# Weight sums of the last down projection: accumulating DMAs from GpSimd's queue in place of VectorE, and two forms swapped

## Chip, cores and metric

The kernel runs on one core of one Trainium2 chip. The metric is the device time of one execution in microseconds, the median of the runs shown. All arithmetic is float32: a matmul operand is split into a rounded part ("hi", float32r) and the remainder ("lo", float32r), and every product is three matmuls (hi·hi, lo·hi, hi·lo).

## What is computed

```python
# x: (8, 128, 512), that is 1024 tokens of width 512
def _L0_cond_ref(...):                       # F = 1376, LoRA of rank 16 per batch entry
    gate = lora_add(einsum('bnh,fh->bnf', x, W_gate), x, A_gate, B_gate)
    up = lora_add(einsum('bnh,fh->bnf', x, W_up), x, A_up, B_up)
    return lora_add(einsum('bnf,hf->bnh', silu(gate) * up, W_down), act, A_down, B_down)
def _L0_ffn_ref(x, ln_w, gate_w, up_w, down_w):   # I = 1792
    nx = x * rsqrt(mean(x * x) + 1e-5) * ln_w
    g, u = nx @ gate_w.T, nx @ up_w.T
    return (silu(g) * u) @ down_w.T
x = x + _L0_ffn_ref(_L0_cond_ref(x, ...), ...)
```

Only the last line of `_L0_ffn_ref`, the product with `down_w`, is touched by the change.

## The kernel before

Channels stand on the 128 partitions and tokens along the free axis, in two halves of 512. Every large product is done by a Strassen-Winograd scheme: seven products of blocks in place of eight, for which sums of weight blocks and sums of activation blocks are made first. The program is one hand-written instruction stream for each engine, synchronised by semaphores, and each engine takes its stream strictly in the order written. In outline: gate and up of the first stage (groups `j` of 0 to 9), its down projection, the norm, gate and up of the second stage (groups `j` from `S1` on, in `group(j, ...)`), and last the down projection of the second stage.

The last down projection is a row of 49 *items* on TensorE, seven products of seven (`KF`) items; item `i` belongs to product `i // 7` and has `k = i % 7`. An item is six matmuls of 128x512: two output tiles by three passes. `DOWN` names each product's activation form, the number of its weight form, and its PSUM banks. Products 0, 5 and 6 use weight blocks as loaded (`vj_in`, tile `jraw`); products 1 to 4 (`nt1`, `nt2`, `22`, `t3`) use sums of blocks, of which there are four forms for each `k`, held in the tile `vs`.

How the forms of one `k` come to be: SP loads four blocks (512 KB) into `vraw`, a view of the tile `wdr` (`load_v`, L356). VectorE makes the four forms in place, four dependent additions of 128x256 (`sums_v`, L1012). ScalarE writes the rounded part of all four, 128x1024, to `vs` (`hi_v`, through the helper of L415), and VectorE the remainder (`lo_v`, through the helper of L889). There is one `vraw`, so the load of the next `k` waits for `lo_v` of the one before. This happens seven times, in the order `V_ORDER`. The first five of them lie in the groups of gate and up: `sums_v` in one group, `hi_v` on ScalarE at the same group's end, `lo_v` in the next group. The sixth ends among the first items, and the seventh (`k` = 6) is written out like this:

```python
                if i == 2 * KF - 1:
                    hi_v(KF - 1)        # ScalarE, behind its work for item 13
...
                elif i == 2 * KF - 1:
                    sums_v(KF - 1)      # VectorE, behind its work for item 13
                    lo_v(KF - 1)
```

TensorE waits for the `lo` of that `k` at the items of product 1 (`s_vlo`), so item 13 is the first to use the seventh set. Behind `hi_v(KF - 1)` stand on ScalarE `copy_q1()` and the rounded operand of item 14 (`hi_down(14)`); behind `lo_v(KF - 1)` stand on VectorE the sum (`down_sum("nt2", 0)`, L1035) that `hi_down(14)` reads, and the remainder `lo_down(14)`. Item 14 waits for both. `load_v(KF - 1)` stands on SP behind `lo_v` of the sixth set; `copy_u2()` puts two PSUM banks into `wdr` much later.

GpSimd makes a mask and a few zeros in the first part of the program and has nothing after that.

Of the kernel before, what the change touches and what calls it, by code (L numbers as in the profile page):

```python
# [16 lines left out]
P = 128  # L17
# [6 lines left out]
S1, S2 = G1 - 2, G2 - 2  # L24
# [7 lines left out]
KF = FF // 2  # L32
# [6 lines left out]
V_ORDER = (4, 5, 0, 1, 2, 3, 6)  # L39
# [2 lines left out]
RING_F = (X11, XT1, XT2, X21, X22, XT3, XT4)  # L42


def build(nc, xT_in, idx_in, wsh_in, w0_in, wgu_in, wd_in, vs_in, vj_in, agu_in, bgu_in, ad_in, bd_in, lnw_in, out):
    f32, f32r, i32 = mybir.dt.float32, mybir.dt.float32r, mybir.dt.int32
    ALU, ACT = mybir.AluOpType, mybir.ActivationFunctionType
    ds = bass.ds
    ctx = ExitStack()
    with ctx:  # L50
# [3 lines left out]
        def sem(name):  # L54
            return ctx.enter_context(nc.semaphore(name))
# [78 lines left out]
        DA_BANK, DB_BANK, DG_BANK = [bank[3], bank[7]], [bank[0], bank[2]], [bank[5], bank[1]]  # L134
# [25 lines left out]
        vraw = wdr[:, :, :].rearrange("p a n -> p (a n)").rearrange("p (c m) -> p c m", m=256)  # L160
# [9 lines left out]
        def act_at(f, t):  # L170
            return act[:, f, t * CH:(t + 1) * CH]
# [5 lines left out]
        def slot_f(u, part):  # L177
            s = u % 14
            return xs[:, RING_F[s // 2], part, s % 2, :]

        DOWN = (("11", None, 0, DA_BANK), ("nt1", 3, None, DG_BANK), ("nt2", 1, None, DB_BANK), ("22", 2, None, DG_BANK),
                ("t3", 0, None, DB_BANK), ("21", None, 1, DA_BANK), ("t4", None, 2, DB_BANK))

        def down_op(i):
            name, k = DOWN[i // KF][0], i % KF
            return act_at(k + KF if name in ("21", "22") else k, 0 if name in ("11", "t3", "21") else 1)

        def down_w(i, part):
            form, j = DOWN[i // KF][1:3]
            return vs[:, i % KF, form, part, :] if j is None else ws[:, j % 2, i % KF, part, :]  # L190
# [11 lines left out]
        def w_of(g):  # L202
            return g + 2
# [57 lines left out]
        s_var, s_rs, s_nw, s_nx = sem("var_done"), sem("rsqrt_done"), sem("refine_steps"), sem("nx_done")  # L261
        s_ug, s_uu, s_us, s_um = sem("unit_gate"), sem("unit_up"), sem("unit_silu"), sem("unit_act")
        s_z, s_pre, s_res = sem("last_product"), sem("residual_with_copy"), sem("residual_added")
        s_v_ld, s_vsum, s_vhi, s_vlo = sem("v_loaded"), sem("v_sums"), sem("v_hi"), sem("v_lo")
        s_j_ld, s_jhi, s_jlo = sem("j_loaded"), sem("j_hi"), sem("j_lo")
        s_dsum, s_dca, s_dcm, s_dcu = sem("down_sums"), sem("down_q1_copied"), sem("down_g_copied"), sem("down_u2_copied")

# [126 lines left out]
        def _(pool):  # L394
# [14 lines left out]
            pool.wait_ge(s_stklo, 8)  # L409
            nc.gpsimd.memset(ad[:, :, :, RANK:2 * RANK], 0.0).then_inc(s_ad_pad, 1)  # L410

        @block.scalar
        def _(a):
            def copy(out_ap, in_ap, scale=1.0):
                return nc.scalar.activation(out_ap, in_ap, ACT.Copy, scale=scale)  # L415
# [135 lines left out]
                copy(wdc[:, n, 0, :], wdr[:, n % 2, :]).then_inc(s_wdhi, 1)  # L551

            def hi_v(k):
                a.wait_ge(s_vsum, 4 * k + 4)
                copy(vs[:, V_ORDER[k], :, 0, :], vraw).then_inc(s_vhi, 1)

            def hi_j(n):
# [31 lines left out]
            def hi_down(i):  # L589
                name, k = DOWN[i // KF][0], i % KF  # L590
                if name in ("11", "22", "21"):
                    a.wait_ge({"11": s_c11[1], "22": s_c22f, "21": s_c21[1]}[name], S1 // 2 + k + 1)
                else:
                    a.wait_ge(s_dsum, ("nt1", "nt2", "t3", "t4").index(name) * KF + k + 1)
                if i >= 14:
                    a.wait_ge(s_use, 11 + i - 13)
                elif i % 2 == 0:
                    a.wait_ge((s_q1, s_g, s_p6, s_q2, s_p3, s_p7, s_p4)[i // 2], S2)
                copy(slot_f(i, 0), down_op(i)).then_inc(s_ahi, 1)
# [267 lines left out]
            for i in range(2, 7 * KF):  # L867
                p = i // KF
# [18 lines left out]
        def _(v):  # L887
            def sub(out_ap, raw, part):
                return nc.vector.tensor_tensor(out_ap, raw, v32(part), ALU.subtract)  # L889
# [83 lines left out]
            def stack_lo(c, t):  # L973
                v.wait_ge(s_stkhi, 4 * c + 2 * t + 2)
                part = (slice(2 * t, 2 * t + 2), slice(0, CHUNK[c]))
                sub(stk[c % 2][32:64, part[0], part[1]], raw[c % 2][0:32, part[0], part[1]],
                    stk[c % 2][0:32, part[0], part[1]]).then_inc(s_stklo, 1)
# [26 lines left out]
                v.wait_ge(s_wdhi, n + 1)  # L1004
                sub(wdc[:, n, 1, :], wdr[:, n % 2, :], wdc[:, n, 0, :]).then_inc(s_wdlo, 1)

            def sums_v(k):
                v.wait_ge(s_v_ld, 16 * (k + 1))
                for q, (to, more) in enumerate(((3, 0), (0, 1), (1, 3), (2, 1))):
                    if q >= 1:  # L1010
                        v.wait_ge(s_vsum, 4 * k + q)
                    nc.vector.tensor_tensor(vraw[:, to, :], vraw[:, to, :], vraw[:, more, :], ALU.add).then_inc(s_vsum, 1)  # L1012

            def lo_v(k):
                v.wait_ge(s_vhi, k + 1)
                v.wait_ge(s_vsum, 4 * k + 4)
                part = vs[:, V_ORDER[k]]
                sub(part[:, :, 1, :], vraw, part[:, :, 0, :]).then_inc(s_vlo, 1)

# [28 lines left out]
            def lo_down(i):  # L1048
                name, k = DOWN[i // KF][0], i % KF
                v.wait_ge(s_ahi, 22 + i + 1)  # L1050
                if name in ("nt1", "nt2", "t3", "t4"):
                    v.wait_ge(s_dsum, ("nt1", "nt2", "t3", "t4").index(name) * KF + k + 1)
                sub(slot_f(i, 1), down_op(i), slot_f(i, 0)).then_inc(s_alo, 1)
# [131 lines left out]
            def group(j, first, last):  # L1185
                if j > first:
                    if j not in (1, S1 + 2, S1 + 3):
                        c22_sum(j - 1)
                    if 1 <= j < 7:
                        stack_lo((j - 1) // 2 + 2, (j - 1) % 2)  # L1190
                    if j % 2 == 0:
                        c22_act(j - 1)
                if w_next(j) < last:
                    sums(w_of(w_next(j)))
                if j > S1 + 2 and j % 2 == 0:
                    lo_v((j - S1) // 2 - 2)
                elif j > S1 + 2:
                    sums_v((j - S1) // 2 - 1)
                if j > first and j % 2 == 0:
                    c21(j - 1)  # L1200
                if w_next(j) < last:
                    lo_a(w_of(w_next(j)))
                    if j == 0:
                        x_sum(0, 3)
                    elif j == S1 + 2:
                        c12(j)
                        c22_sum(j)
                    lo_b(w_of(w_next(j)))
                if j == 0:
                    c22_sum(0)  # L1210
                    lo_t(0, 3)
                if j >= S1 and j % 2 == 0:
                    down_sum("nt1", (j - S1) // 2 - 1)
                if j == S2 - 1:
                    lo_down(0)
                    lo_down(1)
                    lo_j(0)
                    lo_j(1)
                if j == S1 - 1:
                    lo_wd(0)  # L1220
                    lo_ac(0)
                if j % 2 == 1 and j != S1 + 3:
                    c11(j)
                if j != S1 + 2:
                    c12(j)
# [91 lines left out]
            for i in range(2, 7 * KF):  # L1317
                p, k = i // KF, i % KF
                if i % KF == 0 and p == 4:
                    for h in range(4):  # L1320
                        with_copy(h, *((s_dcu, du2, ALU.add) if h < 2 else (s_dcm, dm5, ALU.subtract)))
                elif i % KF == 0 and p == 5:
                    for h in range(2):
                        residual(h, 3, DG_BANK, ALU.add, False)
                elif i % KF == 0 and p == 6:
                    for h in range(2, 4):
                        residual(h, 4, DB_BANK, ALU.subtract, False)
                if p in (2, 4, 6) and k == 0:
                    down_sum(("nt2", "t3", "t4")[p // 2 - 1], 0)
                if p in J_AT:  # L1330
                    lo_j(KF * J_AT.index(p) + k)
                if p in (2, 4, 6) and k + 1 < KF:
                    down_sum(("nt2", "t3", "t4")[p // 2 - 1], k + 1)
                lo_down(i)
                if i == 3:
                    c22_act(S2 - 1)
                elif i == 4:
                    c21(S2 - 1)
                elif i == 5:
                    lo_v(KF - 2)  # L1340
                elif i == KF - 1:
                    down_sum("nt1", KF - 1)
                elif i == 2 * KF - 1:
                    sums_v(KF - 1)
                    lo_v(KF - 1)
            for h in range(2):
                residual(h, 5, DA_BANK, ALU.add, True)
# [9 lines left out]
        def _(pe):  # L1357
# [343 lines left out]
            def down_item(i, tiles=range(2)):  # L1701
                p, k = i // KF, i % KF
                for h in tiles:
                    for s, r in PASSES:
                        ins = mm(DOWN[p][3][h][:, :], down_w(i, s)[:, h * P:(h + 1) * P], slot_f(i, r),  # L1705
                                 start=(p < 2 and k == 0 and s == 0 and r == 0),
# [108 lines left out]
```

## Time and profile before

| | us |
|---|---|
| Median of 3 runs | 396.95 (396.59 to 397.47) |
| Span of the profiled execution | 395.5 |
| Runs' median less that span | 1.45 |
| TensorE busy | 391.8 |
| VectorE busy | 314.8 |
| ScalarE busy | 240.8 |
| GpSimd busy | 10.6 |

The profile is of one execution; its own time is known as its span, from the first instruction to the last, and the median of the runs stands 1.45 us above it. Sums below are made on the span and carried over to the median. Matmuls are pipelined and their ends are modelled, so that busy 99% of the span means that the profile shows no gap between matmuls, not that the array is at its peak.

### The profile page before, as it was taken

The numbers are of one execution on the slowest core, as the hardware profiler recorded it, in microseconds if no ns is written. First come the engines' busy times: TensorE is split into PE (matmuls) and PEld (weight loads), VectorE is DVE, ScalarE is ACT, GpSimd is POOL, SyncE is SP. The second block draws the span as 40 slices with busy tenths as digits, with TensorE's granted clock in tenths as the row PEclk, the third lists the DMA queues.
The fourth block names the chain that finished last, engine by engine and source line by source line (L and its number), as shares of the span: only waits on it lengthen the run. The fifth ranks groups of instructions, "written<-read, shape, count | busy, mean of one in ns | idle before, by whom it ended". The sixth has DMA issues, their size and how long they took to land.

```text
span 395.5 us, 5733 instructions
## 1 busy us (share of the span) xinstructions
PE 391.8 (99%) x1984; PEld 327.3 (83%) x1984; DVE 314.8 (80%) x476; ACT 240.8 (61%) x386; POOL 10.6 (3%) x13
## 2 busy tenths in 40 slices
PE   9999999999999999999999999999999999999997
PEld 5899888888888888888888888888888888888885
DVE  4899979586835869578699787878787869899994
ACT  5969786857574469815745656464646494484740
POOL 6300000000000000000000000000000000000000
PEclk9999999999999999999999999999999999999999
DMA  7640243311111551000400021313130316105112
GB/s 271 182 133 0 83 133 98 110 53 55 53 55 54 164 154 57 2 0 0 159 2 1 12 97 55 106 53 108 60 119 37 89 57 199 55 1 201 54 53 108
DMA packets 14942, 32.42 MB, mean 82 GB/s; under 512 B 2370, under 2 KB 4930, under 8 KB 14914
## 3 DMA queue, kind: packets, MB, share of 16 engines
q1 hardware_dynamic: 13792, 30.22, 23.7%
q10 hardware_dynamic: 1122, 1.84, 1.3%
q8 instruction: 16, 0.26, 0.3%
q14 instruction: 12, 0.10, 0.1%
HBM read 29.95 MB, written 2.10 MB: 81 GB/s over the span
## 4 chain that ended last, share of the span: by engine, by line
PE 99%; DVE 0%; issue 0%; DVEq 0%
PE bank L1365 53%; PE bank L1705 17%; PE bank L1593 14%; PE bank L1511 3%; PE bank L1557 3%; PE bank L1546 3%; PE bank L1375 3%; PE bank L1615 1%; PE bank L1607 1%; PE bank L1505 1%; PE bank L1714 0%; PE bank L1622 0%; DVE act L1354 0%; DVEq L1352 0%
## 5 line engine op out<-in xcount | busy, mean ns | idle before, releaser
L1365 PE MATMUL bank<-xs,ws 128*128 128x512 f32 x840 | 195.0, 390 | 0.0
L1365 PEld LDWEIGHTS bank<-xs,ws 128*128 128x128 f32 x840 | 156.6, 188 | 31.9
L415 ACT ACTIVATE xs<-act 128x512 fp32r<-128x512 f32 x71 | 42.8, 623 | 21.1 <-DVE act L1045 7.6
L1593 PE MATMUL bank<-xs,wdc 128*128 128x512 f32 x240 | 55.7, 390 | 0.0
L1593 PEld LDWEIGHTS bank<-xs,wdc 128*128 128x128 f32 x240 | 44.8, 188 | 9.5 <-issue 0.2
L889 DVE TENSOR_TENSOR xs<-act,xs 128x512 fp32r<-128x512 f32 x71 | 47.5, 685 | 2.7 <-ACT xs L415 2.1
L889 DVE TENSOR_TENSOR ws<-wraw,ws 128x256 fp32r<-128x256 f32 (+2 forms) x45 | 30.0, 668 | 13.0 <-ACT ws L415 12.8
L415 ACT ACTIVATE bank<-bank 128x512 f32<-128x512 f32 x30 | 17.3, 580 | 34.5 <-PE bank L1365 33.7
L415 ACT ACTIVATE mu<-bank 128x512 f32<-128x512 f32 x44 | 26.1, 596 | 20.1 <-PE bank L1365 13.6
L1705 PE MATMUL bank<-xs,vs 128*128 128x512 f32 x168 | 38.2, 389 | 0.0
L1705 PEld LDWEIGHTS bank<-xs,vs 128*128 128x128 f32 x168 | 31.5, 188 | 6.5
L889 DVE TENSOR_TENSOR ws<-wsum,ws 128x1024 fp32r<-128x1024 f32 x20 | 24.5, 1225 | 12.0 <-ACT ws L415 12.0
L415 ACT ACTIVATE ws<-wraw 128x256 fp32r<-128x256 f32 (+2 forms) x44 | 26.8, 614 | 7.8 <-PE bank L1365 3.3
L1705 PE MATMUL bank<-xs,ws 128*128 128x512 f32 x120 | 27.7, 389 | 0.0
L1705 PEld LDWEIGHTS bank<-xs,ws 128*128 128x128 f32 x120 | 22.5, 188 | 4.7
L415 ACT ACTIVATE stack<-bgu_raw 32x1024 fp32r<-32x1024 f32 (+1 forms) x20 | 22.7, 1137 | 0.3
L415 ACT ACTIVATE ws<-wsum 128x1024 fp32r<-128x1024 f32 x20 | 21.1, 1055 | 2.3 <-DVE wsum L903 2.3
L487 ACT ACTIVATE act<-bank 128x512 f32<-128x512 f32 (+1 forms) x28 | 16.3, 596 | 9.3 <-PE bank L1375 6.8
L1365 PE MATMUL bank<-xs,wx 128*128 128x512 f32 x84 | 19.7, 389 | 0.0
L1365 PEld LDWEIGHTS bank<-xs,wx 128*128 128x128 f32 x84 | 15.8, 188 | 3.3
L889 DVE TENSOR_TENSOR wdc<-wdr,wdc 128x512 fp32r<-128x512 f32 x10 | 6.9, 687 | 11.4 <-ACT wdc L415 11.4
L889 DVE TENSOR_TENSOR stack<-bgu_raw,stack 32x1024 fp32r<-32x1024 f32 (+1 forms) x10 | 13.2, 1322 | 2.9 <-ACT stack L415 2.7
(133 smaller groups left out, 439.5 us busy)
## 6 DMA issues: line engine op xcount, KB each, us to landing
wraw<-wgu_in SPq DMA_DIRECT2D x22, 512.0 KB, 3.3
wdr<-vs_in SPq DMA_DIRECT2D x7, 512.0 KB, 3.6
wraw<-vj_in SPq DMA_DIRECT2D x3, 896.0 KB, 4.7
wdr<-wd_in SPq DMA_DIRECT2D x10, 256.0 KB, 2.7
xa<-xT_in SPq DMA_DIRECT2D x4, 256.0 KB, 4.1
xa<-xT_in ACTq DMA_DIRECT2D x2, 512.0 KB, 4.7
bgu_raw<-bgu_in SPq DMA_DIRECT2D x32, 32.0 KB, 1.9
xres<-xT_in SPq DMA_DIRECT2D x4, 256.0 KB, 3.5
```

The costliest lines, as they stand in the source:

```text
L415: return nc.scalar.activation(out_ap, in_ap, ACT.Copy, scale=scale)
L487: return nc.scalar.activation(out_ap, in_ap, ACT.Silu, scale=scale)
L889: return nc.vector.tensor_tensor(out_ap, raw, v32(part), ALU.subtract)
L1365: ins = mm(z[:, :], w_slot(j)[:, w, s, k * P:(k + 1) * P], xs[:, c, r, k, :], start=(start and k == 0 and s == 0 and r == 0), stop=(k == 1 ...
L1375: ins = mm(z[0:m, half], stk[c % 2][:, 2 * t + q, cols], t_op[:, half], start=(alone and q == 0), stop=(q == 1), skip_group_check=True)
L1505: mm(B_BANK[i % 2][:, :].rearrange("p (k n) -> p k n", k=KT), one, one.unsqueeze(1).to_broadcast([P, KT, P]), start=True, stop=True)
L1511: mm(UNIT_BANK[i][g][:, cols], w0_tile(s, k, g, i), x_op(k, 0, r)[:, cols], start=(k == 0 and s == 0 and r == 0 and cols.start == 0), stop ...
L1546: mm(UNIT_BANK[n][g][:, :], w0_tile(s, k, g, UNITS[n][0]), x_op(k, 1, r), start=(k == 0 and s == 0 and r == 0), stop=(k == KT - 1 and s == ...
L1557: ins = mm(SHORT_BANK[t][g][:, half], wsh[s][:, k, g, q, :], x_op(k, t, r)[:, half], start=(k == 0 and s == 0 and r == 0 and q == 0), stop ...
L1593: ins = mm(z[:, :], wd[:, s, h * P:(h + 1) * P], x[r], start=(start and s == 0 and r == 0), stop=False, skip_group_check=True)
L1607: ins = mm(T_BANK[t][32 * b:32 * b + 32, tokens], ad[:, 2 * t + b // 2, n, col:col + 2 * RANK], act_at(ORDER_C[n], t)[:, tokens], start=(n ...
L1705: ins = mm(DOWN[p][3][h][:, :], down_w(i, s)[:, h * P:(h + 1) * P], slot_f(i, r), start=(p < 2 and k == 0 and s == 0 and r == 0), stop=(s ...
```

## The change

GpSimd takes over the weight sums. The host feeds a second array, `vmore_in`, three blocks (384 KB) for each `k`. After `load_v` has landed, GpSimd issues a DMA that adds these three blocks onto the first three of `vraw`, waits for it, and issues a second DMA that adds `vraw`'s second block, read twice, onto its third and fourth (256 KB written). The second DMA's semaphore is what `hi_v` and `lo_v` now wait for. `sums_v` and its three calls are gone from VectorE. The four forms stand in another order in `vraw`, so `nt1` uses form 1 and `nt2` form 3.

```diff
-        DOWN = (("11", None, 0, DA_BANK), ("nt1", 3, None, DG_BANK), ("nt2", 1, None, DB_BANK), ("22", 2, None, DG_BANK),
+        DOWN = (("11", None, 0, DA_BANK), ("nt1", 1, None, DG_BANK), ("nt2", 3, None, DB_BANK), ("22", 2, None, DG_BANK),
...
+            for k in range(KF):
+                pool.wait_ge(s_v_ld, 16 * (k + 1))
+                nc.gpsimd.dma_start(vraw[:, 0:3, :], vmore_in[V_ORDER[k]].rearrange("p (a m) -> p a m", a=3), accum_op=ALU.add
+                                    ).then_inc(s_vsum[0], 16)
+                pool.wait_ge(s_vsum[0], 16 * (k + 1))
+                nc.gpsimd.dma_start(vraw[:, 2:4, :], vraw[:, 1:2, :].to_broadcast([P, 2, 256]), accum_op=ALU.add
+                                    ).then_inc(s_vsum[1], 16)
...
             def hi_v(k):
-                a.wait_ge(s_vsum, 4 * k + 4)
+                a.wait_ge(s_vsum[1], 16 * (k + 1))
...
-            def sums_v(k):
-                v.wait_ge(s_v_ld, 16 * (k + 1))
-                for q, (to, more) in enumerate(((3, 0), (0, 1), (1, 3), (2, 1))):
-                    if q >= 1:
-                        v.wait_ge(s_vsum, 4 * k + q)
-                    nc.vector.tensor_tensor(vraw[:, to, :], vraw[:, to, :], vraw[:, more, :], ALU.add).then_inc(s_vsum, 1)
...
                 elif i == 2 * KF - 1:
-                    sums_v(KF - 1)
                     lo_v(KF - 1)
...
-        "vs_in": np.stack([blocks[b] for b in ((1, 0), (0, 0), (0, 1), (1, 1))], 2).reshape(KF, P, 4 * 256),
+        "vs_in": np.stack([blocks[b] for b in ((1, 0), (1, 1), (0, 1), (0, 0))], 2).reshape(KF, P, 4 * 256),
+        "vmore_in": np.stack([blocks[b] for b in ((0, 0), (1, 0), (0, 0))], 2).reshape(KF, P, 3 * 256),
```

VectorE's stream where the seventh set is made, before. The first row is the sum for item 13, the seven rows behind it are the remainders of items 7 to 13, and the rows of L1035 and what follows are sum and remainder for items 14 and on.

```order
L1030 TENSOR_TENSOR act<-act 128x512 [waits c12_act,c11_act]
L889 TENSOR_TENSOR xs<-act,xs 128x512 [waits down_sums,act_hi] x7
L1012 TENSOR_TENSOR wdr<-wdr 128x256 [waits v_loaded]
L1012 TENSOR_TENSOR wdr<-wdr 128x256 [waits v_sums] x3
L889 TENSOR_TENSOR vs<-wdr,vs 128x4x256 [waits v_sums,v_hi]
L1035 SCALAR_TENSOR_TENSOR act<-act 128x512 [waits c22_act,act_lo,act_hi] x2
L889 TENSOR_TENSOR xs<-act,xs 128x512 [waits down_sums,act_hi]
```

The same place of VectorE's stream in the changed kernel.

```order
L897 TENSOR_TENSOR xs<-act,xs 128x512 [waits act_hi]
L1031 TENSOR_TENSOR act<-act 128x512 [waits c12_act,c11_act]
L897 TENSOR_TENSOR xs<-act,xs 128x512 [waits down_sums,act_hi] x7
L897 TENSOR_TENSOR vs<-wdr,vs 128x4x256 [waits v_sums,v_hi]
L1036 SCALAR_TENSOR_TENSOR act<-act 128x512 [waits c22_act,act_lo,act_hi] x2
L897 TENSOR_TENSOR xs<-act,xs 128x512 [waits down_sums,act_hi]
```

The four additions are gone; nothing else on VectorE has changed its place. The remainder of the seventh set still stands ahead of everything for item 14, and its wait is now for a DMA.

GpSimd's stream in the changed kernel, from its last zeros on; before, it ended with the row of L410.

```order
L410 MEMSET ad 128x44x16 [waits stack_lo]
L414 DMA wdr<-vmore_in 128x768 [waits v_loaded]
L417 DMA wdr<-wdr 128x2x256 [waits v_sums_of_two]
L414 DMA wdr<-vmore_in 128x768 [waits v_loaded]
L417 DMA wdr<-wdr 128x2x256 [waits v_sums_of_two]
```

The pair of DMAs stands there seven times, and each DMA waits for the one before it to land.

## Rows read from the trace of the kernel before

**Rows 1.** The page: span, and busy time of each engine with its count of instructions.

```profile
span 395.5 us, 5733 instructions
PE 391.8 (99%) x1984; PEld 327.3 (83%) x1984; DVE 314.8 (80%) x476; ACT 240.8 (61%) x386; POOL 10.6 (3%) x13
```

**Rows 2.** Waits of TensorE, all of them: us in total, times, longest us.

```profile
PE bank L1505 <- PEq L1808: 0.8, 1, 0.8
```

**Rows 3.** The chain that ended last, in order of time: start us, us, what.

```profile
0.85 3.57 PE bank L1505 x8
...
194.71 129.95 PE bank L1365 x573
324.65 2.72 PE bank L1705 x12
...
328.73 62.56 PE bank L1705 x276
391.29 1.44 PE bank L1714 x12
```

**Rows 4.** Instructions on tile `wdr`: duration min/median/max ns, first and last start.

```profile
L1012 DVE TENSOR_TENSOR wdr<-wdr x28: 417/424/427, 226.4 to 338.7; 128x256 f32<-128x256 f32 x28
```

**Rows 5.** Timeline from 233 us, one of the first sets: start, us, what, [idle before].

```profile
233.66 0.33 SPq L356 DMA_DIRECT2D wdr<-vs_in  x1
...
241.14 1.79 DVE L1012 TENSOR_TENSOR wdr<-wdr 128x256 f32<-128x256 f32 x4
...
245.89 1.05 ACT L415 ACTIVATE vs<-wdr 128x1024 fp32r<-128x1024 f32 x1
...
249.89 0.58 ACT L415 ACTIVATE bank<-bank 128x512 f32<-128x512 f32 x1 [2.95 <-PE bank L1365]
```

**Rows 6.** SP's queue from 185 us: start, us, what.

```profile
237.81 9.85 SPq L282 DMA_DIRECT2D wraw<-wgu_in  x2
```

**Rows 7.** Timeline from 331 us, the seventh set: start, us, what, [idle before].

```profile
331.56 0.33 SPq L356 DMA_DIRECT2D wdr<-vs_in  x1
...
331.93 25.49 SPq L370 DMA_DIRECT2D wraw<-vj_in  x2
...
337.29 1.81 DVE L1012 TENSOR_TENSOR wdr<-wdr 128x256 f32<-128x256 f32 x4
339.13 1.06 ACT L415 ACTIVATE vs<-wdr 128x1024 fp32r<-128x1024 f32 x1 [5.39 <-DVE wdr L1012]
...
340.22 1.23 DVE L889 TENSOR_TENSOR vs<-wdr,vs 128x1024 fp32r<-128x1024 f32 x1 [1.13 <-ACT vs L415]
...
342.08 1.24 ACT L415 ACTIVATE xs<-act 128x512 fp32r<-128x512 f32 x2 [0.93 <-DVE act L1035]
342.75 0.69 DVE L889 TENSOR_TENSOR xs<-act,xs 128x512 fp32r<-128x512 f32 x1
```

**Rows 8.** DMAs issued, whole span: KB each, median us from issue to landing.

```profile
wdr<-vs_in SPq DMA_DIRECT2D x7, 512.0 KB, 3.6
wraw<-vj_in SPq DMA_DIRECT2D x3, 896.0 KB, 4.7
wdr<-wd_in SPq DMA_DIRECT2D x10, 256.0 KB, 2.7
...
act<-xT_in SPq DMA_DIRECT2D x4, 256.0 KB, 6.2
out<-xres SPq DMA_DIRECT2D x4, 256.0 KB, 2.0
```

**Rows 9.** DMAs issued from 325 to 345 us, same columns.

```profile
wraw<-vj_in SPq DMA_DIRECT2D x1, 896.0 KB, 8.9
wdr<-vs_in SPq DMA_DIRECT2D x1, 512.0 KB, 5.7
```

**Rows 10.** Stretches of the span: busy by engine (PE, PEld, DVE, ACT, POOL), PEclk, DMA share, GB/s.

```profile
337.29:339.10 1.81, 1.81 (x10) 1.50 (x9) 1.70 (x4) 0.00 (x0) 0.00 (x0) 1.00 0.28 112
...
395.00:395.50 0.50, 0.00 (x0) 0.00 (x0) 0.00 (x0) 0.00 (x0) 0.00 (x0) 0.50 0.00 0
```

More of the change, by code:

```diff
@@ L42, with build @@
 RING_F = (X11, XT1, XT2, X21, X22, XT3, XT4)
-def build(nc, xT_in, idx_in, wsh_in, w0_in, wgu_in, wd_in, vs_in, vj_in, agu_in, bgu_in, ad_in, bd_in, lnw_in, out):
+def build(nc, xT_in, idx_in, wsh_in, w0_in, wgu_in, wd_in, vs_in, vmore_in, vj_in, agu_in, bgu_in, ad_in, bd_in, lnw_in, out):
     f32, f32r, i32 = mybir.dt.float32, mybir.dt.float32r, mybir.dt.int32
@@ L263, in build @@
         s_z, s_pre, s_res = sem("last_product"), sem("residual_with_copy"), sem("residual_added")
-        s_v_ld, s_vsum, s_vhi, s_vlo = sem("v_loaded"), sem("v_sums"), sem("v_hi"), sem("v_lo")
+        s_v_ld, s_vsum, s_vhi, s_vlo = sem("v_loaded"), [sem("v_sums_of_two"), sem("v_sums")], sem("v_hi"), sem("v_lo")
         s_j_ld, s_jhi, s_jlo = sem("j_loaded"), sem("j_hi"), sem("j_lo")
@@ L1005, in lo_wd @@
                 sub(wdc[:, n, 1, :], wdr[:, n % 2, :], wdc[:, n, 0, :]).then_inc(s_wdlo, 1)
-            def sums_v(k):
-                v.wait_ge(s_v_ld, 16 * (k + 1))
-                for q, (to, more) in enumerate(((3, 0), (0, 1), (1, 3), (2, 1))):
-                    if q >= 1:
-                        v.wait_ge(s_vsum, 4 * k + q)
-                    nc.vector.tensor_tensor(vraw[:, to, :], vraw[:, to, :], vraw[:, more, :], ALU.add).then_inc(s_vsum, 1)
             def lo_v(k):
                 v.wait_ge(s_vhi, k + 1)
-                v.wait_ge(s_vsum, 4 * k + 4)
+                v.wait_ge(s_vsum[1], 16 * (k + 1))
                 part = vs[:, V_ORDER[k]]
@@ L1196, in group @@
                     lo_v((j - S1) // 2 - 2)
-                elif j > S1 + 2:
-                    sums_v((j - S1) // 2 - 1)
                 if j > first and j % 2 == 0:
```

## The prediction

> **What bounds the kernel.** I read the page first. TensorE is busy 391.8 of 395.5 us, VectorE 314.8, ScalarE 240.8, GpSimd 10.6 [rows 1]. The list of TensorE's waits has one entry, 0.8 us at the very start [rows 2]. The chain that ended last is TensorE's own stream: 573 matmuls in 129.95 us and 276 in 62.56 us, 0.2267 us each in both [rows 3]. So TensorE is never starved, and VectorE's load is not what the end waits for. Work taken off VectorE is worth nothing as long as that is so, and whatever makes TensorE wait is added whole, because no idle time behind it can absorb it.
>
> That turns the question into one of spare time: by when must each set of weight sums be there, and how much later does it come from two DMAs than from VectorE?
>
> **What is removed.** 28 additions of 0.424 us [rows 4], 11.9 us of VectorE in seven portions of 1.8 us. By the paragraph above this gives 0.0 on TensorE. The swap of forms 1 and 3 reads another slice of the same tile and costs nothing; all four forms of a `k` come from one ScalarE copy and one VectorE subtraction, before and after.
>
> **What is added, the first six sets.** Call C the time from the landing of `vs_in` to the landing of the second accumulating DMA. For the second set the load is issued at 233.66 and lands 3.6 later at its median [rows 5, 8], at about 237.3. ScalarE's copy of the sums starts at 245.89 [rows 5]. So C up to 8.6 us changes nothing at all. Behind the copy ScalarE has 2.95 us in which it waits for TensorE before its next copy, the one at 249.89 [rows 5], so C up to 11.6 is absorbed there. That next copy is awaited by TensorE only after two more products of six matmuls (2.72 us less the copy's 0.58, about 2.1), so TensorE itself first waits at C of some 13.7. The sets 3 to 5 repeat this pattern, the first is loaded during the norm, long before its sums at 226.4 [rows 4], and the sixth ends among items whose operands are made ahead. One thing works against it here: SP issues another weight load at 237.81 [rows 6], 512 KB, which runs on beside the first accumulating DMA. A load of that size takes 3.6 alone [rows 8], so sharing costs at most about that: with C of 8.6 it would be 12.2, still under 13.7. I cost these six at nothing; the cover is ScalarE's wait for TensorE.
>
> **What is added, the seventh set.** Here the cover is thin. An item is 6 x 0.2267 = 1.36 us. Item 2 begins at 328.73 [rows 3], so item 13 begins at 328.73 + 11 x 1.36 = 343.69 and item 14 at 345.05. Now [rows 7]: the load goes out at 331.56, VectorE's sums start at 337.29 when it has landed (5.7 us later [rows 9]), and end at 339.10; ScalarE copies at 339.13; VectorE's remainder runs 340.22 to 341.45, and item 13 may start, 2.24 us early. But item 14's operand is queued behind on both engines: its sum, ScalarE's copy at 342.08, VectorE's remainder at 342.75 to 343.44. That is 1.61 us ahead of item 14. From there on the chain makes an operand in 1.2 us, faster than TensorE's 1.36, so item 14 is the tightest place.
>
> The load's landing does not move: it is issued when the sixth set's remainder is done, and that stands behind work that waits for TensorE. So with C = 1.81 now, TensorE's stall is S = C - 1.81 - 1.61 = C - 3.42, of which C - 4.05 falls ahead of item 13 and up to 0.63 ahead of item 14.
>
> **How long is C?** No DMA of GpSimd's queue and no accumulating one is in this trace, so I bound it. *Below:* as if both were plain loads of SP. 256 KB take 2.7, 512 KB 3.6 [rows 8], 384 KB between them 3.15; together 5.85, S = 2.4. *Above:* 256 KB took 6.2 in a crowded moment, and 512 KB 5.7 [rows 8, 9]; one of each gives 11.9, S = 8.5. *Between:* an accumulating DMA also reads its destination. If that costs like twice the bytes, 384 KB become 768, between 512 at 3.6 and 896 at 4.7, so 4.3; 256 become 512, 3.6; with SP's issue time of 0.33 [rows 7] once for each, C = 8.6 and S = 5.2. I take this. The other end's cause is partly present: the 896 KB load issued at 331.93 lands only after 8.9 us, at 340.8 [rows 7, 9], and the DMA engines are still 28% busy from 337.29 to 339.10 [rows 10].
>
> The Trainium skill (DMA: Bandwidth & Descriptors, Anatomy of one DMA) fits a DMA from GpSimd as 2.0 us plus its bytes at 436 GB/s. By it the two would take 2.9 and 2.6, an estimate of C = 5.5 and S = 2.1; its figure for 256 KB agrees with the trace's 2.7, and it says nothing of accumulation.
>
> **The clock.** In the last half microsecond of the span the granted clock is 0.50, the level of 1.2 GHz [rows 10]; the last matmul ended at 391.29 + 1.44 = 392.73 [rows 3], so the clock fell within 2.3 us of idleness there. With C = 8.6 the idle time ahead of item 13 is 4.55 us, longer than that. The nearest price for coming back is the program's start, where 8 matmuls took 3.57 us, 0.446 each [rows 3], in place of 1.81 at 0.2267: 1.76 lost. Of that the 0.63 us which TensorE would wait ahead of item 14 anyway is absorbed, leaving 1.1. I add it. The Trainium skill (TensorE: Matmul & The Clock Gate, Why this matters for your kernels) has the rule that idle gaps between bursts of matmuls put the clock back to its lower level; the fall at the end of this span agrees.
>
> **Sum.** 0.0 for VectorE, 0.0 for six sets, 5.2 for the seventh, 1.1 for the clock: +6.3 us. On the profiled span 395.5 gives 401.8; on the median, 1.45 higher, 396.95 gives 403.3.
>
> **Rivals.**
>
> *The chain is longer than every cover* (10%). If an accumulating DMA of these sizes takes 7 us or more, C passes 13.7 in the groups too, where the load at 237.81 adds to it. At C = 15 in the groups each of the five sets 2 to 6 costs 1.3, together 6.5; the seventh costs 15 - 3.42 + 1.1 = 12.7; that gives 416. For it: nothing in the trace prices accumulation. Against: no load in [rows 8] has a median above 6.2.
>
> *No slower* (8%). The turning point is C = 3.4, or 4.2 if 0.2% (0.8 us, about what a measurement of this kernel can tell from no change) is allowed. The shortest landing for 256 KB is 2.0, a store [rows 8]; two DMAs at that speed make C = 4.0, a stall of 0.6 and 397.5. Against it: loads of the same size take 2.7, and there are two in a row here. A gain proper would need TensorE to have waited for VectorE, which its list of waits excludes [rows 2]; I leave 2% of the 8 for it, at 396.
>
> *Same chain, clock stays up* (within the forecast's 82%). If the gap ends before the clock falls, the sum is 5.2 and the time 402.2. If the DMAs are as quick as plain loads, the idle time ahead of item 13 is 1.8, shorter than the 2.3 at the span's end, and the time is 396.95 + 2.4 = 399.4.
>
> **Numbers.** Forecast 82% (the seventh set alone stalls, C from 5.85 to 12 or so), its own range 399.4 to 406.6 (8.5 + 1.1 above). The long chain has 10%; to leave out no more than two in ten I carry the upper end a little into the space between the two, to 409.5, and the lower end to 399.2. Slower 92%, within 0.2% 6%, faster 2%.
>
> **What would show it.** VectorE's rows of L1012 gone, its busy time down by about 12 us. Two GpSimd DMAs seven times, some 4 to 5 us from issue to landing each. ScalarE's copies to `vs` in the groups later by under 3 us, with no new wait on TensorE before 343 us. The seventh copy near 346, waiting for a DMA; TensorE's first wait inside the program at item 13, 4 to 5 us long, a shorter one at item 14; a granted clock below 1.00 behind it. I am wrong if TensorE waits in the groups (C above 13.7), if C is under 4.2, or if the load's landing at 337.29 moves.

## The result

The changed kernel takes 403.61 us (402.48 to 405.64, 5 runs) where the one before took 396.95: 1.0168 times as long, 95% interval 1.0142 to 1.0195. The forecast was 403.3. The profiled execution was the longest of the five, 405.64 with a span of 403.9; the other spans are 400.8 to 401.9. In the experiments two single executions far above all others of their kernel are left out as slow ones (1422.6 us in run 3, and 661.93 us in run 4, at a mean granted clock of 0.559).

The page of the changed kernel: span, busy time, two rows of the 40 slices, GpSimd's DMA queue, and the two new DMAs with KB each and median us to landing.

```profile
span 403.9 us, 5719 instructions
...
PE 393.7 (97%) x1984; PEld 328.6 (81%) x1984; DVE 303.6 (75%) x448; ACT 241.0 (60%) x386; POOL 25.7 (6%) x27
...
PE   9999999999999999999999999999999999399997
...
PEclk9999999999999999999999999999999999699999
...
q0 software_dynamic: 2912, 4.59, 6.9%
...
wdr<-vmore_in POOLq DMA_DIRECT2D x7, 384.0 KB, 5.8
...
wdr<-wdr POOLq DMA_DIRECT2D x7, 256.0 KB, 3.6
```

VectorE lost the 28 additions and 11.2 us [rows 1, 4], while GpSimd gained 15.1 us to issue the DMAs (10.6 before). TensorE has one slice in 40 (10.1 us each) in which it is busy for about a third, and in the same slice PEclk falls. The waits of TensorE, all of them (us in total, times, longest us), answer to [rows 2]:

```profile
PE bank L1703 <- DVE vs L897: 6.5, 1, 6.5
PE bank L1503 <- PEq L1807: 0.9, 1, 0.9
```

One new wait, for VectorE's remainder of the seventh set, at item 13. The timeline there, answering to [rows 7] (start, us, what, idle before; L423 and L897 are the helpers that were L415 and L889):

```profile
331.65 0.33 SPq L356 DMA_DIRECT2D wdr<-vs_in  x1
...
337.82 0.92 POOL L414 DMA_DIRECT2D wdr<-vmore_in  x1 [15.17 <-DMA wdr<-vs_in]
343.92 1.22 POOL L417 DMA_DIRECT2D wdr<-wdr  x1 [5.18 <-DMA wdr<-vmore_in]
347.59 1.06 ACT L423 ACTIVATE vs<-wdr 128x1024 fp32r<-128x1024 f32 x1 [13.76 <-DMA wdr<-wdr]
...
348.68 1.23 DVE L897 TENSOR_TENSOR vs<-wdr,vs 128x1024 fp32r<-128x1024 f32 x1 [11.30 <-ACT vs L423]
...
350.05 25.17 PE L1703 MATMUL bank<-xs,vs 128*128 128x512 f32 x102 [6.52 <-DVE vs L897]
```

C is read off here: the load has landed when GpSimd starts at 337.82, the second DMA has landed when ScalarE starts at 347.59, so C = 9.8 us. Item 12 ended at 343.53, item 13 begins at 350.05. In stretches of 1 us (busy of PE, PEld, DVE, ACT, POOL, then PEclk, DMA share, GB/s):

```profile
346.00:347.00 1.00, 0.00 (x0) 0.00 (x0) 0.00 (x0) 0.00 (x0) 0.00 (x0) 0.99 1.24 199
347.00:348.00 1.00, 0.00 (x0) 0.00 (x0) 0.00 (x0) 0.41 (x1) 0.00 (x0) 0.50 0.09 11
...
352.00:353.00 1.00, 1.00 (x4) 0.81 (x3) 1.00 (x2) 0.47 (x1) 0.00 (x0) 0.50 0.00 0
353.00:354.00 1.00, 1.00 (x4) 0.77 (x4) 1.00 (x3) 0.43 (x2) 0.00 (x0) 0.59 0.00 0
354.00:355.00 1.00, 1.00 (x6) 0.83 (x5) 1.00 (x3) 0.43 (x2) 0.00 (x0) 1.00 0.00 0
```

The granted clock is at 0.50, the 1.2 GHz level, from 347.0 to 353.8, and from 350.05 on matmuls run at it: 4 in a microsecond, not 6. The groups show the other half of the story, a chain with cover. The second set, answering to [rows 5]:

```profile
237.24 0.94 POOL L414 DMA_DIRECT2D wdr<-vmore_in  x1 [35.23 <-DMA wdr<-vs_in]
...
243.88 1.21 POOL L417 DMA_DIRECT2D wdr<-wdr  x1 [5.70 <-DMA wdr<-vmore_in]
...
247.66 1.06 ACT L423 ACTIVATE vs<-wdr 128x1024 fp32r<-128x1024 f32 x1 [1.82 <-DMA wdr<-wdr]
249.73 0.58 ACT L423 ACTIVATE bank<-bank 128x512 f32<-128x512 f32 x1 [1.01 <-PE bank L1363]
```

C is 10.4 here. ScalarE's copy comes 1.8 us late, its next wait for TensorE is 1.01 in place of 2.95, and TensorE notices nothing. The sixth set has a longer chain:

```profile
314.01 0.93 POOL L414 DMA_DIRECT2D wdr<-vmore_in  x1 [10.70 <-DMA wdr<-vs_in]
...
321.45 1.21 POOL L417 DMA_DIRECT2D wdr<-wdr  x1 [6.51 <-DMA wdr<-vmore_in]
...
325.11 1.06 ACT L423 ACTIVATE vs<-wdr 128x1024 fp32r<-128x1024 f32 x1 [2.31 <-DMA wdr<-wdr]
```

C is 11.1 there, and 9.7 to 11.4 over sets 2 to 6: the first DMA takes 6.1 to 7.4 us in these places and the second 3.6 to 4.4.

### The profile page after: what moved, and what is told of

It is laid out like the page before. It is cut to its first block, busy times and chain, and to the rows that moved or that the text cites. A ratio compares the mean times of both kernels' runs of the same rounds, so it can differ in the third digit from the quotient of the medians.

```text
span 403.9 us, 5719 instructions
## 1 busy us (share of the span) xinstructions
PE 393.7 (97%) x1984; PEld 328.6 (81%) x1984; DVE 303.6 (75%) x448; ACT 241.0 (60%) x386; POOL 25.7 (6%) x27
## 4 chain that ended last, share of the span: by engine, by line
PE 87%; DMA 6%; issue 3%; DVE 2%; ACT 1%; POOL 0%; DVEq 0%; ACTq 0%; POOLq 0%
PE bank L1363 46%; PE bank L1591 14%; PE bank L1703 12%; PE bank L1509 3%; PE bank L1555 3%; PE bank L1544 3%; PE bank L1373 3%; DMA wdr<-vs_in 2%; DMA wdr<-wdr 2%; DMA wdr<-vmore_in 2%; PE bank L1613 1%; PE bank L1605 1%; DVE vs L897 1%; PE bank L1503 1%; PE bank L1712 0%
## 5 line engine op out<-in xcount | busy, mean ns | idle before, releaser
L423 ACT ACTIVATE xs<-act 128x512 fp32r<-128x512 f32 x71 | 42.8, 623 | 19.0 <-DVE act L1046 7.6
L897 DVE TENSOR_TENSOR xs<-act,xs 128x512 fp32r<-128x512 f32 x71 | 47.6, 687 | 4.6 <-ACT xs L423 4.0
L1703 PE MATMUL bank<-xs,vs 128*128 128x512 f32 x168 | 40.3, 402 | 6.5 <-DVE vs L897 6.5
L897 DVE TENSOR_TENSOR ws<-wraw,ws 128x256 fp32r<-128x256 f32 (+2 forms) x45 | 30.0, 669 | 19.8 <-ACT ws L423 19.7
L1703 PEld LDWEIGHTS bank<-xs,vs 128*128 128x128 f32 x168 | 32.8, 196 | 13.9 <-issue 6.9
L423 ACT ACTIVATE mu<-bank 128x512 f32<-128x512 f32 x44 | 26.1, 596 | 19.5 <-PE bank L1363 13.0
L897 DVE TENSOR_TENSOR ws<-wsum,ws 128x1024 fp32r<-128x1024 f32 x20 | 24.5, 1225 | 12.0 <-ACT ws L423 12.0
L423 ACT ACTIVATE bank<-bank 128x512 f32<-128x512 f32 x30 | 17.3, 580 | 26.8 <-PE bank L1363 25.9
L423 ACT ACTIVATE ws<-wraw 128x256 fp32r<-128x256 f32 (+2 forms) x44 | 26.8, 614 | 7.8 <-PE bank L1363 3.3
L423 ACT ACTIVATE stack<-bgu_raw 32x1024 fp32r<-32x1024 f32 (+1 forms) x20 | 22.7, 1137 | 0.3
L423 ACT ACTIVATE ws<-wsum 128x1024 fp32r<-128x1024 f32 x20 | 21.1, 1054 | 2.5 <-DVE wsum L911 2.5
L423 ACT ACTIVATE vs<-wdr 128x1024 fp32r<-128x1024 f32 x7 | 7.4, 1062 | 25.0 <-DMA wdr<-wdr 25.0
L414 POOL DMA_DIRECT2D wdr<-vmore_in x7 | 6.6, 942 | 206.1 <-DMA wdr<-vs_in 206.1
```

What stands on the lines that cost most here:

```text
L414: nc.gpsimd.dma_start(vraw[:, 0:3, :], vmore_in[V_ORDER[k]].rearrange("p (a m) -> p a m", a=3), accum_op=ALU.add).then_inc(s_vsum[0], 16)
```

## The experiments

All were timed against the kernel before on the chip they ran on; ratios are to that, with 95% intervals. Times are medians. The recorded ratios agree with means over the executions other than the profiled one, so they can differ by some 0.2% from the ratio of two medians.

**1. The seventh set back on VectorE.** GpSimd keeps the first six.

```diff
-            for k in range(KF):
+            for done, k in enumerate(k for k in range(KF) if k not in ON_DVE):    # ON_DVE = (6,)
...
+                elif j > S1 + 2:
+                    sums_v((j - S1) // 2 - 1)          # does nothing unless k is in ON_DVE
...
                 elif i == 2 * KF - 1:
+                    sums_v(KF - 1)
                     lo_v(KF - 1)
```

> GpSimd's DMAs make the first six sets of weight sums, VectorE's four additions the seventh, in the block order of before. Theory (only the seventh set is exposed): the whole loss is gone, 396.9 us within 0.8 of before, no wait on TensorE inside the program. Rival (the first six sets, their DMA traffic or ScalarE's later copies cost too): 398 us or more, with a wait or longer matmul spacing between 226 and 343 us.

396.80 against 397.22, ratio 0.9993 (0.9984 to 1.0002). TensorE's only wait is the 0.9 us at the start. The whole loss is in the seventh set, and the six others cost nothing that shows.

**2. Only the seventh set on GpSimd.** The same kernel with `ON_DVE = (0, 1, 2, 3, 4, 5)`.

> VectorE makes the first six sets, GpSimd's DMAs only the seventh. Theory: the loss of the whole change, 402.5 to 404.5 us, one wait of about 5 to 6.5 us on TensorE at item 13. Rival (several sets share the loss): clearly less, 400 us or under.

405.02, ratio 1.0197 (1.0182 to 1.0212), a little above the range that I gave; its interval overlaps that of the changed kernel on another chip (run 9, 1.0155 to 1.0202). One wait on TensorE, 4.8 us; the clock is low behind it for longer than in the changed kernel, to 354.7.

```profile
342.50 1.20 POOL L423 DMA_DIRECT2D wdr<-wdr  x1 [4.24 <-DMA wdr<-vmore_in]
346.16 1.06 ACT L429 ACTIVATE vs<-wdr 128x1024 fp32r<-128x1024 f32 x1 [12.27 <-DMA wdr<-wdr]
...
348.62 3.75 PE L1721 MATMUL bank<-xs,vs 128*128 128x512 f32 x8 [4.78 <-DVE vs L903]
```

**3. The gap filled with matmuls.** Into bank 4, which no one uses between the gate and up products and the last items.

```diff
                 pe.wait_ge(s_alo, 22 + i + 1)
+                if i == 2 * KF - 1:
+                    pe.wait_ge(s_c21[0], S2 // 2)
+                    pe.wait_ge(s_c21[1], S2 // 2)
+                    for n in range(20):
+                        mm(bank[4][:, :].rearrange("p (k n) -> p k n", k=KT), one,
+                           one.unsqueeze(1).to_broadcast([P, KT, P]), start=True, stop=True)
```

> The changed kernel with 20 extra bf16 matmuls of 512 columns (4.3 us at full clock) that TensorE issues into an unused bank ahead of its wait for the seventh set; nothing else is different. Theory (the gap also costs a fall of the clock): granted clock 1.00 behind the gap, time down by 1.1 to 1.9 us against the changed kernel, so 401.7 to 402.5. Rival (the clock's fall costs nothing measurable, the wait is all): 403.6 as the changed kernel.

403.85, ratio 1.0158 (1.0137 to 1.0179): not faster than the changed kernel's 403.61, which had run on another chip. The mean granted clock was 1.00, so the fall was prevented and yet the time hardly moved. So I ran it again later, beside the changed kernel (9 and 10).

**4. The seventh set loaded early.** Into `wsum`, free once the last gate and up weights are made, instead of `wdr`.

```diff
+        vraws = [vraw] * (KF - 1) + [wsum[:, :, :]]
...
                 if j == 0:
+                    load_v(KF - 1)      # waits for the load before to land, not for lo_v
                     sp.wait_ge(s_c22f, S2 // 2)
...
-                    load_v(KF - 1)
```

> All seven sets by GpSimd's DMAs, but the seventh is loaded into the tile that held the gate and up sums (free from about 314 us on), some 17 us earlier, so that its chain of DMAs is over long before item 13. Theory (the DMAs cost only what their chain is late): 396.9 us within 0.8 of before, no wait on TensorE. Rival (the DMAs themselves slow something, or the seventh chain delays the sixth): 398 or more.

397.41 against 397.22, ratio 1.0005 (0.9996 to 1.0014), no wait on TensorE in the program. All fourteen DMAs are there and cost nothing that shows.

```profile
329.71 1.22 POOL L420 DMA_DIRECT2D wsum<-wsum  x1 [4.79 <-DMA wsum<-vmore_in]
...
336.15 1.06 ACT L426 ACTIVATE vs<-wsum 128x1024 fp32r<-128x1024 f32 x1 [1.01 <-DMA wsum<-wsum]
...
338.60 1.22 DVE L900 TENSOR_TENSOR vs<-wsum,vs 128x1024 fp32r<-128x1024 f32 x1
```

Two things qualify this. The load went out at 314.33, 17 us earlier, but the chain began only at 323.47, because GpSimd issued the sixth set's second DMA just before (322.77). And the chain itself took 12.7 us, from 323.47 to 336.15: its 256 KB DMA alone took 6.4 us, with SP's four 256 KB loads and the 896 KB load issued at 329.35 to 333.30 beside it. An accumulating DMA of the same shape took 3.6 to 3.7 for the seventh set elsewhere.

**5 and 6. Plain copies in place of accumulation, from GpSimd and from SP**, for the seventh set alone. Both kernels leave out that set's sums.

```diff
-                nc.gpsimd.dma_start(vraw[:, 0:3, :], vmore_in[...]..., accum_op=ALU.add
+                nc.gpsimd.dma_start(vraw[:, 0:3, :], vmore_in[...]...        # run 5, k == KF - 1; the second likewise
...
+                    sp.wait_ge(s_v_ld, 16 * KF)                              # run 6, on SP
+                    sp.dma_start(vraw[:, 0:3, :], vmore_in[V_ORDER[KF - 1]].rearrange("p (a m) -> p a m", a=3)).then_inc(s_vsum[2], 16)
+                    sp.wait_ge(s_vsum[2], 16)
+                    sp.dma_start(vraw[:, 2:4, :], vraw[:, 1:2, :].to_broadcast([P, 2, 256])).then_inc(s_vsum[3], 16)
```

> The changed kernel, in which the two DMAs of the seventh set, still from GpSimd's queue and of the same shapes, copy in place of adding (so that set's sums are left out). If accumulation is what makes C (9.8 us in the changed kernel's trace) longer than plain loads, C falls to about 6.5 to 7.5 and the time to 400 to 401; if GpSimd's queue is, C stays above 9 and the time at 403 to 404.

> As the run before, but the two plain copies of the seventh set are issued by SP (its sums are left out here too). By the lower bound of the prediction C is 5.9 us, the stall 2.4 and the time 399.4. If C is 5.9 here and 9 or more from GpSimd without adding, the queue is the cost; if both are near 6, adding is.

Run 5 took 402.18, ratio 1.0119 (1.0068 to 1.0170), run 6 400.68, ratio 1.0104 (1.0067 to 1.0141). The timelines of 5, then of 6:

```profile
337.57 0.61 POOL L415 DMA_DIRECT2D wdr<-vmore_in  x1 [15.28 <-DMA wdr<-vs_in]
341.86 0.72 POOL L418 DMA_DIRECT2D wdr<-wdr  x1 [3.68 <-DMA wdr<-vmore_in]
344.31 1.06 ACT L424 ACTIVATE vs<-wdr 128x1024 fp32r<-128x1024 f32 x1 [10.85 <-DMA wdr<-wdr]
```

```profile
334.88 0.33 SPq L379 DMA_DIRECT2D wdr<-vmore_in  x1
339.25 0.71 SPq L381 DMA_DIRECT2D wdr<-wdr  x1
341.81 1.06 ACT L428 ACTIVATE vs<-wdr 128x1024 fp32r<-128x1024 f32 x1 [8.50 <-DMA wdr<-wdr]
```

C is 6.7 from GpSimd and 6.9 from SP, so in one trace of each GpSimd's queue adds nothing that shows; adding does. Counted from the start of its issue to the start of what waits for it, the first DMA takes 4.3 and 4.4 as a copy and 5.2 to 6.1 accumulating, the second 2.5 and 2.6 against 3.6 to 3.7. (From issue to landing alone, the first copy took 3.8 from GpSimd and 4.4 from SP; GpSimd's next issue then came 0.5 us after the landing, SP's at once.) Run 6 is nearer to the kernel before than run 5 in this trace mostly because its seventh load had landed after 3.7 us, where it took 4.9 to 6.0 in the other traces with the same loads around it (changed kernel, 1, 2, 3, 5, 9 and 10), but for 4.4 and 3.5 in runs 7 and 8; its four executions spread over 4 us (398.69 to 403.02).

**7 and 8. Longer chains in the groups**, the seventh set on VectorE as in run 1. The first DMA is cut in two (7), or both are cut to 128 KB pieces, five in all (8), each waiting for the one before.

```diff
+                for q in range(2):
+                    to = slice(q, 3 if q == 1 else q + 1)
+                    nc.gpsimd.dma_start(vraw[:, to, :], more[:, to, :], accum_op=ALU.add).then_inc(s_vsum[0], 16)
+                    pool.wait_ge(s_vsum[0], 16 * (2 * done + q + 1))
```

> The seventh set on VectorE; in the first six the first accumulating DMA is cut in two that wait for each other (256 + 128 KB), so that C in the groups grows from 10.4 to about 14 us. The prediction's bound for a wait on TensorE is 13.7: so at most a few tenths of a us for each of five sets, 396.9 to 398.5. A cover of only ScalarE's wait (11.6) would give 2.4 for each of five sets, about 409.

> As the run before, with five accumulating DMAs for each of the first six sets (3 x 128 KB, then 2 x 128 KB), C about 19 us. With the bound of 13.7 each of five sets stalls TensorE by about 5 us, 420 to 425 in all, clock falls included. If the groups could hide any chain, 397.

Run 7 took 405.70, ratio 1.0207 (1.0190 to 1.0224), well above what I gave. The first cut set in its timeline:

```profile
237.18 0.92 POOL L423 DMA_DIRECT2D wdr<-vmore_in  x1 [31.94 <-DMA wdr<-vs_in]
...
246.80 1.22 POOL L425 DMA_DIRECT2D wdr<-wdr  x1 [3.68 <-DMA wdr<-vmore_in]
...
252.66 1.06 ACT L431 ACTIVATE vs<-wdr 128x1024 fp32r<-128x1024 f32 x1 [6.81 <-DMA wdr<-wdr]
253.62 0.58 ACT L431 ACTIVATE bank<-bank 128x512 f32<-128x512 f32 x1
...
254.25 2.24 PE L1383 MATMUL bank<-xs,ws 128*128 128x512 f32 x5 [1.83 <-ACT bank L431]
```

C is 15.5, not 14: the two pieces of the first DMA took 5.1 and 4.5 us, and the last DMA 5.9, where it took 3.8 in this set of the changed kernel. One of SP's 512 KB weight loads was under way beside it. TensorE waits 1.83 us, for ScalarE's `bank<-bank` copy behind the late one, which is the place that the prediction named; 15.5 less 1.83 is 13.7, its bound. Of the other sets, those with C of 11.6 and 13.0 stall nothing; one with 14.7 stalls 1.81, 0.8 more than the bound gives, and the sixth, with 14.2, shows as 0.7 among the items. The clock fell behind the first stall (0.50 from 256 to 258). So the bound held to within 0.8 us and my estimate of C did not. The waits add up to 4.3 us, of a loss of 8.3 against the kernel before on that chip. The fall of the clock does not explain the rest of the median: it is in the profiled execution alone (mean granted clock 0.996, 405.94 us), while the three others had 1.00 and took 405.06 to 406.09. Their waits may have been longer; some 4 us I cannot place. Run 8 took 422.09, ratio 1.0642 (1.0612 to 1.0672), a total within the expectation. C was 16.1 to 18.3 in sets 2 to 5, not 19, and the stalls behind them 0.55 to 4.24 us, not 5: C less the stall is 12.9 to 15.6, so 13.7 is the second set's figure and not an exact bound for the others. The waits on TensorE, 15.9 us in the program of a loss of 24.7, fall mostly on the same copy, `bank<-bank`; the mean granted clock of 0.984 stands for some 13 us at the lower level (an estimate: twice 0.016 of the span of 419.6), which makes up part of the rest.

```profile
PE bank L1384 <- ACT bank L432: 12.6, 4, 4.2
PE bank L1724 <- DVE xs L906: 3.3, 2, 2.9
```

**9 and 10. The changed kernel, and the filled gap, on one chip.**

> The changed kernel once more, for comparison on one chip with the two runs that follow. 402.5 to 405 us.

> The 20 extra matmuls in the gap once more, now beside the changed kernel on the same chip. In the traces the fall of the clock cost 1.9 us in the changed kernel and 3.0 in the one with only the seventh set on GpSimd. If that is its price in most executions, this is 1.5 to 3 us faster than the run before; if the extra matmuls only trade the slow clock for work of their own, the two are within 0.5.

403.82, ratio 1.0179 (1.0155 to 1.0202), and 403.40, ratio 1.0147 (1.0129 to 1.0165). The extra matmuls gain 0.4 us in median and 1.3 by the ratios, and the intervals overlap. That lies between the two expectations, under 1.5 us and, by the ratios, over 0.5, so it settles neither. The repeated changed kernel waits 4.9 us where the first trace showed 6.5. The filled one:

```profile
343.66 4.54 PE L1742 MATMUL bank<-const-bfloat16-1.0 128*128 128x512 bf16 x20
...
349.08 1.67 PE L1704 MATMUL bank<-xs,vs 128*128 128x512 f32 x6 [0.88 <-DVE vs L898]
351.17 1.17 PE L1704 MATMUL bank<-xs,vs 128*128 128x512 f32 x4 [0.41 <-DVE xs L898]
```

At full clock item 14 waits again, 0.41, for its own operand. At half clock item 13 lasted long enough for that wait to be gone.

**11. SP's other loads out of the way.**

```diff
                 else:
+                    if j == 1:
+                        load_v(KF - 1)
                     sp.wait_ge(s_jlo, KF * j)
+                if j == 1:
+                    sp.wait_ge(s_vsum[1], 16 * KF)
+                    for h in range(4):
+                        sp.dma_start(xres[:, h, :], xT_in[1, h]).then_inc(s_xr_ld[h], 16)
                 sp.dma_start(jraw[:, 0:KF, :], vj_in[j].rearrange("p (k m) -> p k m", k=KF)).then_inc(s_j_ld, 16)
```

> The changed kernel, in which SP issues the four 256 KB loads and the 896 KB load that stand around the seventh load only after its chain of DMAs has landed; nothing else moves. Theory (the seventh load is late because SP's own loads crowd it): it lands in 3.4 to 3.6 us in place of 5.8, C falls to 8.5 to 9.2, the gap on TensorE to about 3 us, the time to 399 to 401. Rival (the chain sets its own pace): gap and time as in the changed kernel.

402.73, ratio 1.0121 (1.0100 to 1.0141); the changed kernel beside it had 1.0179 (1.0155 to 1.0202), so this is a gain of 0.6% by the ratios, whose intervals do not overlap, and of 1.1 us in median, and each execution is below each of run 9; but the time lies above the 399 to 401 that I gave. The seventh load now lands in 3.6 us:

```profile
332.26 0.33 SPq L356 DMA_DIRECT2D wdr<-vs_in  x1
...
336.16 0.92 POOL L417 DMA_DIRECT2D wdr<-vmore_in  x1 [12.95 <-DMA wdr<-vs_in]
341.49 1.22 POOL L420 DMA_DIRECT2D wdr<-wdr  x1 [4.41 <-DMA wdr<-vmore_in]
345.10 1.06 ACT L426 ACTIVATE vs<-wdr 128x1024 fp32r<-128x1024 f32 x1 [10.72 <-DMA wdr<-wdr]
...
347.56 4.81 PE L1706 MATMUL bank<-xs,vs 128*128 128x512 f32 x13 [3.52 <-DVE vs L900]
```

The gap is 3.5 us. C is 8.9 with no other load about, the same as in runs 2 and 9, where the 896 KB load ran on into the chain: at this place the loads around it do not lengthen the chain. (In the groups and in run 4, where they fell otherwise, chains took 9.7 to 12.7.) That they delay the seventh load fits this trace and the shorter time, but two traces speak against it as the only cause: in runs 6 and 8 the same loads stood around it and it landed after 3.7 and 3.5 us. And the clock fell here too, at 348, after TensorE had already gone back to work:

```profile
347.00:348.00 1.00, 0.44 (x2) 0.42 (x3) 1.00 (x3) 0.13 (x1) 0.00 (x0) 1.00 1.01 375
348.00:349.00 1.00, 1.00 (x5) 0.73 (x4) 0.91 (x3) 0.95 (x2) 0.00 (x0) 0.52 1.09 252
```

It did not fall in every execution: in two of the five the mean clock was 1.00, and they took 401.3 and 401.4; the three others (0.991 to 0.996) took 402.7 to 403.1. Whether the clock or a shorter gap made the difference these times alone do not tell.

## Why the prediction was right

**Nothing for VectorE's 11.9 us, nothing for six sets.** Both shown, by run 1 (no loss, no gain) and by the waits of the changed kernel. The spare time was as written: ScalarE's 8.6 and 2.95 us, and behind them TensorE's first wait at C = 13.7, which run 7 measured as 13.7 on its first cut set (12.9 on another, and 12.9 to 15.6 in run 8). What shared the DMA engines in the groups cost less than the 3.6 us allowed for: C was 9.7 to 11.4, still at least 2.3 short of the bound.

**The stall.** S = C - 3.42 was made for a load that lands at 337.29. Corrected for a landing earlier or later (relative to the start of item 2), it can be set against the whole loss behind item 13, read as the later start of the last 12 matmuls (391.13 before), again less the shift of item 2. In us:

| run | C | load late by | S worked out | loss measured | rest | clock behind the gap |
|---|---|---|---|---|---|---|
| changed kernel | 9.8 | 0.7 | 7.0 | 8.6 | 1.5 | fell |
| 2, only the seventh | 8.9 | -0.2 | 5.3 | 7.9 | 2.6 | fell |
| 5, plain from GpSimd | 6.7 | 0.9 | 4.2 | 6.6 | 2.3 | fell |
| 9, changed, again | 8.9 | -0.1 | 5.4 | 7.1 | 1.7 | fell |
| 11, quiet queue | 8.9 | -1.5 | 4.0 | 5.4 | 1.3 | fell |
| 3, gap filled | 8.9 | 0.4 | 5.8 | 6.2 | 0.4 | stayed |
| 6, plain from SP | 6.9 | -1.9 | 1.7 | 2.0 | 0.4 | stayed |
| 10, gap filled, again | 8.8 | 0.5 | 5.9 | 6.3 | 0.4 | stayed |

Where the clock stayed, the formula is 0.4 us short in each of the three; where it fell, 1.3 to 2.6 in each of the five.

**C.** Predicted 8.6 (4.3 and 3.6 as loads of twice the bytes, 0.66 for issuing); measured 9.8 in the profiled execution and 8.8 to 8.9 in five other traces (2, 3, 9, 10 and 11), made of 5.2 to 5.3 and 3.6 to 3.7. The value was close, and 1.2 short in the profiled execution, whose first DMA took 6.1 for a reason that stays open; its derivation held only in part. The second DMA does cost like twice its bytes. The first costs 4.3 already as a plain copy, not the 3.15 interpolated from loads of other sizes, and accumulation adds about 1 us on that. The 896 KB load did not lengthen this chain, by run 11; loads at other moments did (C of 12.7 in run 4). By the Trainium skill's fit for a DMA from GpSimd (DMA: Bandwidth & Descriptors, Anatomy of one DMA) the two were estimated at 2.9 and 2.6. The plain copies of run 5 took 4.3 and 2.5 (3.8 and 2.4 to their landing), so it holds here for the second and not for the first, beside which the 896 KB load was still under way.

**"The load's landing does not move."** This was the weakest step, and the prediction itself named it as a sign of being wrong. The landing varied by more than 2 us between traces (3.5 to 6.0 us after its issue). In the kernel before it could not be seen: VectorE's work for item 13 ended just when the sums began, so landing a little earlier or later was covered on both sides.

**The clock.** It fell as predicted, in each of the five traces with an unfilled gap of 3.5 to 6.5 us. 1.1 us was the price given; the table's rest is 0.9 to 2.2 us above the 0.4 that remains without a fall. That is what it seems to cost in a trace. In the medians, filling the gap gained 0.4 us only (1.3 by the ratios), with overlapping intervals, so how much of the 6.7 us of median loss is the clock's stays open. (Over the ten executions of each that are on record, on different chips in part, the means are 404.0 unfilled and 403.4 filled.) To settle it, the filled and the unfilled kernel would have to be compared at the same C, which varies from one execution to the next. The prediction's own sum, 5.2 and 1.1, has the right total with too much certainty about the parts. In the profiled execution the loss on the span is 8.4, which is 2.1 more than the sum, most of it in the stall (7.0, with C 1.2 longer and the load 0.7 later). The mechanism was right; that the median came within 0.3 us of the forecast is in part luck.

**The rivals.** No set other than the seventh stalls TensorE (runs 1 and 4), so the long chain was not met; run 8 shows what it would have been. C never came near 4.2, at which the change would have been free; the shortest chain, plain copies, took 6.7.

Of the signs named, two were off: the two DMAs were to take 4 to 5 us each and took 5.8 and 3.6 in median, and the shorter wait at item 14 came only in the traces in which the clock stayed up (0.4 us, runs 3, 6 and 10).

No version beats the kernel before: with the stall taken away (runs 1 and 4) the time is its time, since TensorE has no wait left for VectorE's relief to shorten.

## What to carry to other kernels

Work that moves from a compute engine to DMAs relieves that engine and gets longer in latency: 1.8 us of additions became 9 us or more of chained DMAs. It was not less work for the engines as a whole: VectorE lost 11.2 us of busy time, and GpSimd gained 15.1 to issue the DMAs. Before moving such work, list each instance with its own spare time, from the landing of its load to the first wait on the bounding engine; here those in the groups had about 13.7 us and the seventh had 3.4, and the one set the time. The remedy is then an earlier start, in another buffer, for that instance alone (run 4), or leaving that instance where it was (run 1).

## What the runs showed of the hardware

- At the seventh set an accumulating DMA of 256 KB within SBUF took 3.6 to 3.7 us where the plain copy took 2.5; of 384 KB from DRAM, 5.2 to 5.3 (6.1 in one trace) where the copy took 4.3. At other moments, with SP's loads beside them, the same two took up to 6.4 (run 4) and 7.4 (sixth set of the changed kernel).
- A plain copy of the same shape took as long from GpSimd's queue as from SP's, to 0.1 us on either DMA, start of issue to start of what waited for it, in one trace of each (runs 5 and 6). GpSimd itself was busy 0.9 and 1.2 us to issue the two accumulating ones, 0.6 and 0.7 the two plain ones.
- The granted clock stayed at its lower level for about 6.8 us in the changed kernel, during the last 3.8 of which TensorE was already back at work; in run 11 it fell only after the gap of 3.5 us was over.
